# Cross attention and a four-stream mix: four token groups for five, and mixing coefficients loaded and turned once per group

## What is computed

```python
qh = softmax(Wq @ q, over the 64 dims of a head) * SCALE      # 8 heads of 64
kh = softmax(Wk @ ctx, over the 2048 columns)
vh = Wv @ ctx
context = kh @ vh^T ;  out = Wo @ (context^T @ qh) + bo
x = x + out / norm(out over the 256 channels) * g * sqrt(256)
# second part: each of the 4096 rows ("tokens") of x is four streams of 512
logits = rmsnorm(layernorm(x)) @ [W_res, W_pre, W_post]^T + base     # 24 per token
H_res = sinkhorn(logits[:16] / 0.1, 50 rounds)                        # 4x4 per token
H_res = (1 - sigmoid(gate)) * I + sigmoid(gate) * H_res
y = (x_streams weighted by softmax(H_pre)) @ W_branch                 # 512 per token
x = x + H_res @ x_streams + y * softmax(H_post)                       # on the layer norm of x
```

## Time and profile before

| | before |
|---|---|
| time, median of 3 runs | 2599.71 us (2599.68 to 2604.77) |
| the profiled execution's own time | 2600.5 us |
| its span in the trace | 2598.8 us |
| PE busy | 2422.8 us |
| DVE busy | 1764.0 us |
| ACT, POOL busy | 1168.1 us, 1068.3 us |
| mean granted clock of PE, of its full 2.4 GHz | 0.979 |
| moved by DMA | 255.72 MB |

### The profile page before, as it was taken

One profiled execution on the slowest core, in us unless ns is written; L12 is line 12 of the kernel. 1 busy time (PEld: TensorE's weight loads), 2 busy tenths in 40 slices (PEclk: granted clock), 3 DMA queues, 4 the chain that ended last, 5 costly groups with the idle time before them and its releaser, 6 DMA issues.

```text
span 2598.8 us, 35329 instructions
## 1 busy us (share of the span) xinstructions
PE 2422.8 (93%) x12004; PEld 1920.9 (74%) x12004; DVE 1764.0 (68%) x4242; ACT 1168.1 (45%) x2439; POOL 1068.3 (41%) x979
## 2 busy tenths in 40 slices
PE   7999999999999999999999999999999999999864
PEld 6887878787888787777877778777776776777521
DVE  3554645456877777666766768776688786967787
ACT  3454444445453444446454444535445344443332
POOL 1534536271635345362634527262362442624410
PEclk9999999999999999999999999999999999999877
DMA  7112222313123122225334330323424423331265
GB/s 234 49 66 98 73 91 71 99 40 100 60 67 101 57 98 74 89 72 156 98 122 138 97 125 33 105 75 112 127 65 123 132 84 116 98 117 45 80 184 164
DMA packets 200145, 255.72 MB, mean 98 GB/s; under 512 B 43550, under 2 KB 109854, under 8 KB 199966
## 3 DMA queue, kind: packets, MB, share of 16 engines
q1 hardware_dynamic: 199966, 253.47, 31.1%
HBM read 177.53 MB, written 75.89 MB: 98 GB/s over the span
## 4 chain that ended last, share of the span: by engine, by line
PE 64%; DVE 21%; POOL 6%; issue 6%; ACT 3%; DMA 1%; SPq 0%; DVEq 0%; POOLq 0%; ACTq 0%
PE kc_bank L641 15%; PE big L700 10%; PE tb L742 4%; PE big L615 4%; PE tb L627 4%; PE big L617 3%; PE big L616 3%; PE tb L756 3%; PE big L674 3%; PE big L676 3%; PE big L675 3%; PE tb L685 2%; PE misc L722 2%; DVE stats L883 2%; POOL x_tr L1526 2%
## 5 line engine op out<-in xcount | busy, mean ns | idle before, releaser
L1255 ACT COPY turned<-tb 128x512 f32<-128x512 f32 x512 | 298.7, 587 | 754.4 <-PE tb L685 481.6
L700 PE MATMUL big<-merged,turned 128*128 128x256 f32 x2048 | 494.6, 385 | 32.8 <-ACT turned L1255 26.0
L641 PE MATMUL kc_bank<-ctxt,turned 128*128 128x256 f32 x2048 | 480.7, 381 | 0.0
L700 PEld LDWEIGHTS big<-merged,turned 128*128 128x128 f32 x2048 | 386.2, 191 | 107.9 <-ACT turned L1255 22.5
L641 PEld LDWEIGHTS kc_bank<-ctxt,turned 128*128 128x128 f32 x2048 | 376.0, 191 | 53.4 <-issue 10.8
L1484 POOL TENSOR_TENSOR in_l<-x_sb,in_h 128x512 fp32r<-128x512 f32 x128 | 168.7, 1344 | 589.8 <-ACT in_h L1295 589.8
L1509 POOL TENSOR_TENSOR q_sb<-q_sb,qsum 128x1024 f32<-128x1024 f32 x128 | 243.8, 1905 | 281.6 <-DVE qsum L965 281.5
L674 PE MATMUL big<-wq_h,in_h 128*128 128x512 f32 x512 | 238.3, 465 | 16.9 <-DVE q_sb L953 16.4
L856 DVE TENSOR_REDUCE kmax<-big 128x1 f32<-128x512 f32 x256 | 172.3, 685 | 106.3 <-PE big L617 103.5
L615 PE MATMUL big<-in_h,wk_h 128*128 128x512 f32 x512 | 238.0, 465 | 6.4 <-ACT k_exp L1246 6.1
L756 PE MATMUL tb<-mix_ld,mix_w 121*96 121x512 f32 (+2 forms) x324 | 188.9, 680 | 56.4 <-DVE mix_w L1134 26.3
(11 more groups left out here) (148 smaller groups left out, 4490.0 us busy)
## 6 DMA issues: line engine op xcount, KB each, us to landing
mix_ld<-streams SPq DMA_DIRECT2D x157, 240.0 KB
ctxt<-in_ctx_t SPq DMA_DIRECT2D x64, 512.0 KB, 4.3
x_sb<-in_x SPq DMA_DIRECT2D x64, 512.0 KB, 6.2
x_tr<-in_x_t SPq DMA_DIRECT2D x64, 512.0 KB, 6.7
streams<-x_sb SPq DMA_DIRECT2D x64, 512.0 KB, 3.1
stage<-in_ctx SPq DMA_DIRECT2D x60, 512.0 KB, 4.1
out<-mix_out SPq DMA_DIRECT2D x157, 192.0 KB, 2.2
streams<-y_sb SPq DMA_DIRECT2D x32, 256.0 KB, 2.0
```

Of the source, the lines that this page charges most:

```text
L641: t = nc.tensor.matmul(kc_bank[:, 0:C], turned[n % 3][:, j * P:(j + 1) * P], ctxt[:, nt, :], start=nt == 0, stop=nt == NT - 1)
L700: t = nc.tensor.matmul(big[2 + p % 2][:, half], turned[n % 3][:, dt * P:(dt + 1) * P], merged[:, dt, :], start=dt == 0, stop=dt == DT - 1)
L1255: nc.scalar.copy(turned[k % 3][:], tb[n % 2][:]).then_inc(s_tba, 1)
```

## The change

The groups become 5, 5, 4, 2. The biases move into the coefficient tensor as a sixth row per token. Behind a group's Sinkhorn SP stores the coefficients, waits for the store, and loads all of the group's back in two DMAs, one row per tile of 24 tokens, into `stage` (free at that time). ACT sorts them by stream, PE turns them with five transposes into a `tb` bank, ACT copies that to `tile_co`. POOL builds each matrix from a column of it, and the bias is added by ACT's copy out of PSUM (`Identity` with a bias). So the two small loads per tile go; there are four buffers `mix_ld` for five and three `mix_w` for five. The "coefs" task moves to the next place A or B with r of 1 or 2, "sort coefs" 4 and "turn coefs" 5 places behind it; this starts the mixes of a group later. The first loads of the last group are no longer behind its "coefs". In the drain, the next batch's first two key products move ahead by two and three steps, and two `return_pair` move by one.

```diff
-GROUPS = (4, 4, 4, 2, 2)
+GROUPS = (5, 5, 4, 2)
...
-    LOADS, AHEAD = 5, 4
+    LOADS, AHEAD = 4, 4
...
-        put(order_of_places[end + 1], "coefs", gr)
+
+        end += 1
+        while end < len(order_of_places) and (order_of_places[end][0] == "Q" or order_of_places[end][2] not in (1, 2)):
+            end += 1
+        put(order_of_places[end] if end < len(order_of_places) else TAIL, "coefs", gr)
+        put(order_of_places[end + 4] if end < len(order_of_places) else TAIL, "sort coefs", gr)
+        put(order_of_places[end + 5] if end < len(order_of_places) else TAIL, "turn coefs", gr)
         ready.append((end + 1, len(MIX_TILES[gr])))
...
     known += sum(count for _, count in ready)
+    left = known - mixed
+    known += len(MIX_TILES[LAST])
     put_loads(TAIL)
-    left = known - mixed
...
+                nc.sync.dma_start(coef_rows[tokens].rearrange("(t p) s i -> p t s i", p=P),
+                                  coef_all[:, 0:GROUPS[gr] * CT]).then_inc(s_coef, 16)
+                w.wait_ge(s_coef, (gr + 1) * 16)
+                w.wait_ge(s_cl, b * NQ * CT)
...
+                nc.sync.dma_start(come_back[0:full], coef_rows[first - full * TOK:first].rearrange("(k c) s i -> k (c s i)", c=TOK)
+                                  ).then_inc(s_coefld, 16)
...
-                nc.sync.dma_start(mix_co[k][0:count * PARTS, :], coef_rows[tokens].rearrange("c s i -> (c s) i")).then_inc(
-                    s_mixld[k], 16)
-                nc.sync.dma_start(mix_w[k][ONES:ONES + 1, 0:count, :], bias_rows[tokens].rearrange("(a c) i -> a c i", a=1)
...
+                        w.wait_ge(s_sorted, (gr + 1) * 2)
+                        for i in range(STREAMS):
+                            nc.tensor.transpose(bank[0:ROWS, i * TILES:i * TILES + tiles],
+                                                by_stream[0:tiles, i * ROWS:(i + 1) * ROWS], ident[0:tiles, 0:tiles])
...
+                    elif b + 1 < NB and i <= NT:
+                        key_logits(b + 1, 0, i - NT + 1)
+                    elif i in (NT + 1, NT + 3):
+                        return_pair(b, (i - 11) // 2)
...
-                    if b + 1 < NB and i in (17, 19, 21, 23):
-                        key_logits(b + 1, 0, (17, 19, 21, 23).index(i))
-                    if i >= NT and i % 2 == 0 and i < NT + 10:
+                    if b + 1 < NB and i in (21, 23):
+                        key_logits(b + 1, 0, (i - 17) // 2)
+                    if i >= NT + 4 and i % 2 == 0 and i < NT + 10:
...
-                w.wait_ge(s_mixld[k], (n // LOADS + 1) * 48)
                 w.wait_ge(s_const, CONSTS)
+                w.wait_ge(s_tba, SCALAR_READS["coefs", LAST])
+                w.wait_ge(s_tb, TB["mix", n - 3] + 1)
...
-                nc.scalar.copy(mix_out[n % 2][0:rows, :], tb[m % 2][0:rows, :]).then_inc(s_tba, 1)
+                nc.scalar.activation(mix_out[n % 2][0:rows, :], tb[m % 2][0:rows, :], ACT.Identity,
+                                     bias=tile_co[gr % 2][0:rows, STREAMS, at:at + 1]).then_inc(s_tba, 1)
```

More of the change, by code:

```diff
@@ L149, in put_mix @@
         nonlocal made, mixed
-        while made < min(mixed + 2, loaded):
+        while made < min(mixed + 2, loaded, sum(map(len, MIX_TILES[:LAST]))):
             put(place, "matrix", made)
@@ L214, in use_tb_behind @@
                 use_tb(place, "mix", task[1])
+            elif task[0] == "turn coefs":
+                use_tb(place, "coefs", task[1])
     for place in order_of_places:
@@ L262, in xattn_ffn @@
         s_mixld = [sem(f"s_mixld{i}") for i in range(LOADS)]
-        s_coef = [sem(f"s_coef{i}") for i in range(2)]
+        s_coef = sem("s_coef")
+        s_coefld = sem("s_coefld")
+        s_sorted = sem("s_sorted")
         s_yst = [sem(f"s_yst{i}") for i in range(CT)]
@@ L353, in xattn_ffn @@
         mix_ld = [sb(f"mix_ld{i}", [P, COLS]) for i in range(LOADS)]
-        mix_co = [sb(f"mix_co{i}", [P, STREAMS]) for i in range(LOADS)]
-        mix_w = [sb(f"mix_w{i}", [P, TOK, STREAMS]) for i in range(LOADS)]
+        mix_w = [sb(f"mix_w{i}", [P, TOK, STREAMS]) for i in range(3)]
+        tile_co = [sb(f"tile_co{i}", [P, PARTS, TILES]) for i in range(2)]
         mix_mask = sb("mix_mask", [P, TOK])
@@ L489, in behind @@
             def behind(place):
+                nonlocal turning
+                b = place[1] if place != TAIL else NB - 1
                 for task in tasks.get(place, ()):
@@ L754, in behind @@
                             w.wait_ge(s_lastblk, n - last_group + 1)
-                        weights = mix_w[k][0:ONES + 1, 0:count, :].rearrange("p c i -> p (c i)")
-                        t = nc.tensor.matmul(bank[0:count * STREAMS, :], weights, mix_ld[k][0:ONES + 1, :], start=True, stop=True)
+                        weights = mix_w[n % 3][0:count * PARTS, 0:count, :].rearrange("p c i -> p (c i)")
+                        t = nc.tensor.matmul(bank[0:count * STREAMS, :], weights, mix_ld[k][0:count * PARTS, :], start=True,
+                                             stop=True)
+                        t.then_inc(s_tb, 1)
+                    elif task[0] == "turn coefs":
+                        gr = task[1]
+                        tiles = len(MIX_TILES[gr])
+                        bank = take_tb("coefs", gr)
+                        w.wait_ge(s_sorted, (gr + 1) * 2)
+                        for i in range(STREAMS):
+                            nc.tensor.transpose(bank[0:ROWS, i * TILES:i * TILES + tiles],
+                                                by_stream[0:tiles, i * ROWS:(i + 1) * ROWS], ident[0:tiles, 0:tiles])
+                        t = nc.tensor.transpose(bank[0:TOK * STREAMS, STREAMS * TILES:STREAMS * TILES + tiles],
+                                                biases[0:tiles], ident[0:tiles, 0:tiles])
                         t.then_inc(s_tb, 1)
@@ L1024, in sinkhorn @@
                 if gr:
-                    for i in range(2):
-                        w.wait_ge(s_coef[i], gr * 16)
+                    w.wait_ge(s_coef, gr * 16)
                 step(nc.vector.tensor_scalar(skz.rearrange("p t i j -> p t (i j)"), lg[:, logit, 0:RES],
@@ L1397, in behind @@
                         mix_bank(task[1])
+                    elif task[0] == "sort coefs":
+                        sorted_coefs(task[1], place[1] if place != TAIL else NB - 1)
+                    elif task[0] == "turn coefs":
+                        turned_coefs(task[1])
                     elif task[0] == "own first":
@@ L1469, in pool_program @@
                                     pattern=[[PARTS, TOK]], channel_multiplier=-1).then_inc(s_const, 1)
-            for k in range(LOADS):
-                w.wait_ge(s_const, 10)
-                last = nc.gpsimd.memset(mix_ld[k][:], 1.0)
-            last.then_inc(s_const, 1)
-            w.wait_ge(s_const, 11)
             def context_low(b, i, ct):
```

110 lines of the change are left out of this document (67 added, 43 removed).

## The result

The changed kernel takes 2609.62 us (median of 10 runs, 2605.11 to 2612.48), the kernel before 2600.55 us beside it (10 runs, 2599.58 to 2604.77): ratio 1.0028, 95% interval 1.002 to 1.0037. The forecast was 2573. The change costs 9 us where it was to save 27.

What follows compares the result with a forecast made beforehand. PE was taken to bound the plain batches, DVE steps to lengthen the others, and the tail to be another regime (PE busy 83 us, DVE 111). Sum: 2600.5-39-4+4+15-3 = 2573 us; range 2553 to 2592.

Steps and rivals of the forecast that it cites:

- Regrouping body, -39: Batches 4 to 15: the new groups shorten them from 1857.0 to 1817.6 us, -39; bounds -33 and -46.
- Coefficients in the body, +4: Batches 9 and 14: the coefficients' round trips, part hidden, cost +4 us for the two; bounds 0 and 12.
- rival C: Batches 9 and 14: the 53-row return runs on one engine, holding ACT and PE twice; 2580 us; chance 0.17.
- 9.1 us of slack: Batches 9 and 14: time from ACT's last spill copy to the key exponential behind which ACT will wait, 9.1 us.
- Drain, -4: Batch ends: key products moved ahead gain -0.5 us in eight Sinkhorn batches, nothing in plain ones; -4, bounds +3 and -15.
- Tail, first part, +15: Last spill to last Sinkhorn's end: DVE starts 5.4 us late, 65 mixes at 1.65 us; +15, bounds +5.4 and +30.
- The argument that halved issues on SP would help: Tail mixes: two of SP's four issues go; in rival B transfers keep DVE's pace, 2564 us, chance 0.24.
- PE is no limit: 0.85 a mix: Tail mixes: PE needs 0.85 us a mix at the body's full clock, some 1.15 at the tail's mean clock.
- the floor of 1.48: Tail mixes: 432 KB a mix at 266 GB/s, DMA engines 91% busy, sets a floor of 1.48 us.
- Last part, -3: After the last Sinkhorn: eleven mixes end some 34.5 us later instead of 37.4, round trip hidden; -3, bounds 0 and -6.
- D: Tail: a loop so slow, 2.06 us a mix, that it takes back the body's 42 us; slower; chance 0.05.
- A's loop at its upper bound: Tail: rival A has mixes slower than DVE, 2573 us, chance 0.48; the two-output-buffer loop's upper bound is 1.86 us.

Runs made afterwards that it cites:

- the cut return: The changed kernel with the return of full coefficient rows cut into a multiple of 8 rows and the rest (53 as 48 and 5): 2600.92 us, ratio 1.0003.
- groups_alone: The kernel before with only the groups changed to 5, 5, 4, 2; small loads per tile and old drain kept: 2588.78 us, ratio 0.9953.
- the other two edits: The changed kernel with return cut into multiples of 8 rows and third group's sort and turn behind the last Sinkhorn's 13th step, two output buffers: 2593.66 us.
- all_three: The changed kernel with return cut into multiples of 8 rows, three output buffers, third group's sort and turn behind the last Sinkhorn's 13th step: 2579.97 us, ratio 0.9922.
- the later sort: The changed kernel with the third group's sort and turn moved from ahead of the last Sinkhorn to behind its 13th step: 2606.49 us, ratio 1.0021.
- groups_outs3: The kernel before with the new groups 5, 5, 4, 2 and three output buffers: 2587.67 us, ratio 0.9948.
- after_split_outs3: The changed kernel with the return cut into multiples of 8 rows and three output buffers: 2589.05 us, ratio 0.9951.

## Why the prediction was wrong

Three terms of the sum failed, each in one step: the price of a batch with 23 Sinkhorn steps and of the loaded batches behind it (the regrouping), the landing of the 53-row return (the coefficients), and the pace of a mix in the tail. The drain's small gain did not come either.

1. **Regrouping body, -39: direction right, size wrong.** Alone it gave 25.9. The batches that follow are those of the changed kernel. The price of 31 steps of ten tiles held (batches 5 to 7: 438.8 us, forecast 438.3), the plain batch too. Wrong were the batches with 23 steps: I took 3.9 (23/31 of 4.2 us and 1), and it is 6.2 us, as much as for 31. PE waits 3.3 us for `q_sb` there. The trace of before had it: batch 7, 23 steps and 4 mixes, takes

```profile
1026.38:1176.33 149.95, 143.39 (x732) 117.04 (x732) 101.78 (x227) 68.53 (x143) 65.89 (x58) 0.99 0.28 88
```

 that is 149.95 - 140.90 - 4 x 0.85 = 5.65 for 23 steps; I had scaled it from other windows. The two batches make 4.6 us. Then come batches 10 to 12 (3.7) and, of the 15.5 us of batches 9 and 14, the 6.2 that the cut return does not take back; the other terms are near 1 us each (1.8 us are won ahead of batch 4, by which kernels differ there without a cause in the change). Why batches 9 and 14 keep these 6.2 us stays open.

2. **Coefficients in the body, +4: rival C happened.** The 53 rows landed late enough to hold ACT 3.83 and 3.78 us and PE 3.63 and 3.58. Priced at +4 with 0 to 12 as bounds, C at +11; by the last spills of the changed kernel and of the new groups alone (2440.4 and 2430.2) the term was +10.2, near the upper bound. With the cut the last spill is at 2430.4, so the return of 53 rows accounts for nearly all of it. The 9.1 us of slack held: ACT's last copy for the spill ends at 1313.54 in batch 9 and ACT stands still from 1322.7. The store's issue and landing took 4.3 us (1313.97 to 1318.29), as priced. The step that failed is the return's landing, taken as 2.2 to 6.7 us: from its issue to ACT's start it was 8.29, and its packets went one behind the other. By the Trainium skill ("DMA: Bandwidth & Descriptors", on why a DMA increments its semaphore by 16), a slowest dimension of 53 leaves one engine; the traces agree, with at most two packets under way for 53 rows, up to 15 for 42 and up to 17 for 48 and 5. I had named it and given it 0.17, too little: no row spoke against it.

3. **Drain, -4: nothing.** Ratio 0.9997 alone, and 0.2 us between the changed kernel with either drain. That a plain batch gains nothing was right (140.90 both); the gain with Sinkhorn steps was argued, not read.

4. **Tail, first part, +15: mechanism right, size wrong.** The start is 5.5 us late, as forecast (5.4). The step that failed is the pace of a mix: the 65 came at 1.88 us, not 1.65. Of the two bounds I took the middle, though the earlier trace rows had the landing of the tail beside them (2.7), and it gave the upper one. The argument that halved issues on SP would help was wrong: SP was not the limit. groups_alone, with all four DMAs a mix, runs its 61 at 1.86. The loop of the two output buffers was: with a third the stretch loses 7 us alone and 14 beside the other two edits, and then 1.63 is what is measured. Against groups_alone the changed kernel loses 15.7 us in this stretch: 5.8 by the later start, and by my estimate 7.5 by four more mixes at 1.88, since its mixes begin later in the body. Two readings in the forecast were off without deciding it. "PE is no limit: 0.85 a mix" took the growth of a batch for PE's time: two products alone take 1.08 us at the full clock, and PE did come next once the third buffer was in. And the floor of 1.48 took KB as 1000 bytes; it is 1.51.

5. **Last part, -3: about -0.7.** Its mixes pass the same two output buffers; that these held it is not shown (the third gave 1.2 us there in one kernel, 1.8 in another, nothing in all_three). The round trip was hidden, as forecast: DVE's first matrix starts 11.5 us behind ACT's first own-batch activation (2572.73), as it did before.

```profile
2584.24 0.77 DVE L1172 TENSOR_TENSOR mix_w<-mix_mask,tile_co 120x96 f32<-120x96 f32 x3
```

6. **Rivals.** D (slower) gave the result's side but not its way: it wanted 2.06 us a mix with the body's 42 us kept. What happened is A's loop at its upper bound, with C, and with a body that gave 15.7. The misses are of one sign. The range's upper end (2592) was to put C and A's upper pace together; summed up (2600.5 - 39 - 4 + 11 + 30 - 3) that is 2595.5. It left out that the regrouping could give 13 us less and the drain nothing.

By components: the regrouping -13, the return on one engine +9, and +12 more, in the tail (the sum is 8 and the measured loss 9, the difference being that between sets of runs). The third buffer and the later sort give these 12 back in all_three and more. How that divides between these two depends on the order in which they are removed.

## What to carry to other kernels

When per-tile loads are replaced by one load for a group, look at the new load's row count and at who waits in order behind it: 53 rows took 8.3 us, their packets one behind the other, and 42 took 2.3, and two DMAs of 48 and 5 rows removed the wait. When work is moved into a stretch with a steady pace, work out that pace from the loop of the fewest buffers (copy + issue + landing, over the buffers), with the landing measured in that stretch, before any gain on another engine is counted: here it was 1.88 us with two output buffers, and a third brought 7 us by itself and 14 beside the other two edits. Then look at the next limit in turn: here it was PE at the clock that it was granted. And a change that loses as it stands may hold a gain behind one limit: with three small edits the same change is 20 us faster than before.

## What the runs showed of the hardware

A DMA of 53 rows took 8.3 us for 119.2 KB, from its issue to the start of the engine that waited for it, one of 42 rows 2.3 us for 94.5 KB. The 53 packets of 2304 bytes came one every 0.12 us over 6.5 us, the 42 within 0.66 us.

A store of 192 KB landed in 2.2 us over the whole run. Between the last spill and the end of the Sinkhorn it was 2.7 to 2.8 in the kernels with two output buffers; with three it was 3.1 to 3.2 in the changed kernel and its variants with 65 mixes there, and 3.0 in groups_outs3. Over the Sinkhorn 232 to 236 GB/s were moved with two, 243 to 267 with three in the changed kernel: more stores under way landed later each, and the rate still rose. At a DMA share of 0.82 to 0.84 the rate was 232 GB/s with the small loads in it and 267 without, so the share of busy DMA engines was no measure here of the bytes that still fit.

Two products of a mix on PE took 1.08 us at the full granted clock, and four took 3.64 at 0.53. Within every kernel the runs with the higher mean clock tend to be the shorter ones; in after_split_outs3 they go from 2581.11 us at 0.987 to 2592.14 at 0.982.
